# A GNN and FFN kernel: gather ring of 32 tiles, one landing semaphore per block, one ring of one-hots, one PSUM area for the three row parts

## The reference, cut to what matters

```python
x = x + gnn(layernorm(x), src, dst, ...)          # three of these layers, relu between them:
    agg  = segment_sum(h[src], dst, N)            # 200000 gathered rows a layer
    mean = agg / max(deg, 1)
    h    = h @ W_self + mean @ W_neigh + b
x = x + ffn(layernorm(x))                         # gelu(x @ w1 + b1) @ w2 + b2, times a routing
                                                  # weight, for the nodes with the largest weights
```

## Time and profile before

| what | us |
|---|---|
| median of the three runs | 6444.89 |
| the profiled execution, from its first to its last instruction (its span) | 7838.5 |
| POOL busy, of it the gathers | 4678.4, 4576.5 |
| PE busy (matmuls), weight loads | 4641.2, 2616.3 |
| DVE busy | 2368.1 |
| ACT busy | 896.4 |

### The profile page before, as it was taken

The page is one execution under the profiler, slowest core; times in us unless marked ns, Lnnn a source line. Parts: engine busy times, 40 slices in busy tenths (PEclk is TensorE's granted clock), DMA queues, the critical chain, the costliest instruction groups (busy, mean ns, idle before and its releaser), DMA issues.

```text
span 7838.5 us, 97787 instructions
## 1 busy us (share of the span) xinstructions
PE 4641.2 (59%) x19986; PEld 2616.3 (33%) x20208; DVE 2368.1 (30%) x5119; ACT 896.4 (11%) x2129; POOL 4678.4 (60%) x4762
## 2 busy tenths in 40 slices
PE   0445556666777544555555666544556667777884
PEld 0112223333444212222222223212334445555663
DVE  7111222233333211122233333211222233344446
ACT  3000000011111000000000000000111122223331
POOL 5666666666666566666666666666655555555551
PEclk9666677777888766667777777666767788888997
DMA  5444444444454444444445544444444444444444
GB/s 197 136 135 133 134 132 137 132 139 139 140 142 140 129 138 133 140 135 138 138 137 144 143 139 142 134 136 132 131 121 117 115 118 121 119 123 121 126 125 160
DMA packets 460486, 1056.21 MB, mean 135 GB/s; under 512 B 128083, under 2 KB 234279, under 8 KB 460455
## 3 DMA queue, kind: packets, MB, share of 16 engines
q0 software_dynamic: 301056, 925.15, 42.2%
q10 hardware_dynamic: 82364, 97.08, 3.5%
q1 hardware_dynamic: 77035, 33.62, 1.6%
HBM read 971.47 MB, written 84.02 MB: 135 GB/s over the span
## 4 chain that ended last, share of the span: by engine, by line
issue 38%; PE 32%; POOL 10%; another core or an unknown queue 8%; DVE 5%; DMA 2%; DVEq 2%; ACT 1%; SPq 1%; ACTq 0%; POOLq 0%
PE agg L613 12%; POOL gath L504 9%; PE agg_lo L614 6%; PE hid L657 5%; PE y L667 4%; DMA gath<-table,idx_ring 2%; PE hid L553 1%; PE y L553 1%; DVE resid L750 1%; PE hid L578 1%; DVEq L859 1%; DVE onehot L855 1%; DVEq L855 1%; PE agg_lo L603 0%
## 5 line engine op out<-in xcount | busy, mean ns | idle before, releaser
L504 POOL DMA_INDIRECT gath<-table,idx_ring x4704 | 4576.5, 973 | 2923.2 <-issue 1362.3
L613 PE MATMUL agg<-gath,onehot 128*128 x5778 | 2633.4, 478 | 2256.1 <-issue 1759.7
L855 DVE TENSOR_TENSOR onehot<-window_ids,dst_f 128x512 f32 x1464 | 1016.1, 694 | 3949.7 <-PE agg_lo L614 1434.4
L614 PE MATMUL agg_lo<-gath,onehot 128*128 x5856 | 1935.1, 330 | 380.5 <-issue 336.1
L613 PEld LDWEIGHTS agg<-gath,onehot 128*128 x5856 | 662.6, 113 | 3493.9 <-issue 3204.3
L614 PEld LDWEIGHTS agg_lo<-gath,onehot 128*128 x5856 | 660.1, 113 | 760.6 <-issue 576.0
L657 PE MATMUL hid<-featT,w_gnn 128*128 128x128 f32 x3136 | 485.4, 306 | 278.9 <-issue 277.4
L657 PEld LDWEIGHTS hid<-featT,w_gnn 128*128 128x128 f32 x3136 | 449.3, 218 | 311.9 <-issue 306.4
L667 PE MATMUL y<-w_sb,hidT 128*128 128x256 f32 x1568 | 392.5, 408 | 13.9 <-issue 10.9
L667 PEld LDWEIGHTS y<-w_sb,hidT 128*128 128x128 f32 x1568 | 317.1, 208 | 64.0 <-issue 15.1
L1103 ACT ACTIVATE featT<-tp 128x256 f32<-128x256 f32 x196 | 74.2, 379 | 2201.3 <-remote 1540.7
(11 more groups left out here) (129 smaller groups left out, 2462.0 us busy)
## 6 DMA issues: line engine op xcount, KB each, us to landing
gath<-table,idx_ring POOLq DMA_INDIRECT x4704
table<-split ACTq DMA_DIRECT2D x194, 192.0 KB
table<-gath ACTq DMA_DIRECT2D x24, 768.0 KB, 3.6
xb<-x ACTq DMA_DIRECT2D x97, 128.0 KB
yw_dram<-yw ACTq DMA_DIRECT2D x97, 128.0 KB
resid<-x SPq DMA_DIRECT2D x24, 512.0 KB, 7.3
gath<-yw_dram SPq DMA_DIRECT2D x12, 512.0 KB, 7.7
out<-gath ACTq DMA_DIRECT2D x12, 512.0 KB, 9.1
```

Of the source, the lines that this page charges most:

```text
L504: g.indirect_dma_start(gath[:, j, 0:PARTS * D], None, table[layer][:, :], bass.IndirectOffsetOnAxis(ap=idx_ring[:, h, j:j + 1], axis=0)).t ...
L613: mm(hi_mid, oh, tile_rows[:, :, 0:2 * D], start=False, **flags)
L614: last = mm(agg_lo[p][:, 0:lo_cols], oh, tile_rows[:, :, 2 * D:2 * D + lo_cols], start=False, **flags)
L855: v.tensor_tensor(onehot[p][:, bass.ds(slot, GROUP), :], window_ids[p][:].unsqueeze(1).to_broadcast([P, GROUP, P]), dst_f[:, bass.ds(tiles ...
```

## The change

- The ring of gathered rows has 32 slots (8 blocks). `idx_ring` keeps two halves of 16 tiles. `slots_free` starts at 8.
- The four gathers of a block raise one common semaphore, and SP makes one wait a block in place of four.
- The one-hots lie in one ring of 8 places, given out by pair (`(b + n) % 8`) in place of by block and parity. DVE's wait on `slots_free` is for one count more (`b + 2`).
- Each tile has three matmuls of 256 columns (the last 257 in layer 0), all into one PSUM area, in place of one of 512 and one of 256. One matmul with zeros opens the area, in place of two.
- `mean_done` and `aggregate_done` have one operation on the sum in place of three.
- To find room: `w_gnn2` lies in `hidT[0]` and is loaded by ACT after layer 0, ahead of `w1`; PE waits for it ahead of layer 1 (`w2g_loaded`). The 12 `fin` buffers all lie in `gath`; `part`, `trial`, `gains`, `sel` and `flags` lie in other buffers. `dst_f` has 1568 columns in place of 2052, and the last chunk's copy is shorter.

```diff
-RING = 16
+RING = 32
...
-    TURN_TILES = 2 * RING
+    TURN_TILES = RING
+    HALF_TILES = TURN_TILES // 2
+    HALF_BLOCKS = HALF_TILES // GROUP
...
-        onehot = [sb(f"onehot{p}", [P, RING, P], BF16) for p in range(2)]
+        onehot = sb("onehot", [P, RING, P], BF16)
...
+        w_gnn2 = hidT[0][:].rearrange("p k n -> p (k n)").rearrange("p (k n) -> p k n", k=KD)
...
-        agg = [psum(f"agg{p}", [P, 2, D]) for p in range(2)]
-        agg_lo = [psum(f"agg_lo{p}", [P, 512]) for p in range(2)]
+        agg = [psum(f"agg{p}", [P, 512]) for p in range(2)]
...
-                        for j in range(RING):
-                            sp.wait_ge(landed[j], it * 32 + 16 * (2 * layer * TURNS_PER_LAYER + h + 1))
-                            if j % GROUP == GROUP - 1:
-                                sp.sem_inc(rows_ready, 1)
+                        for q in range(h * HALF_BLOCKS, (h + 1) * HALF_BLOCKS):
+                            sp.wait_ge(landed[q], it * (16 * GROUP) + 16 * GROUP * (layer * TURNS_PER_LAYER + 1))
+                            sp.sem_inc(rows_ready, 1)
...
-                mm(hi_mid, zeros[:, 0:P], zeros[:, 0:2 * D], start=True, **free)
-                mm(agg_lo[p][:, 0:lo_cols], zeros[:, 0:P], zeros[:, 0:lo_cols], start=True, **free)
+                mm(agg[p][:, 0:lo_cols], zeros[:], ones_bf[:, 0:lo_cols], start=True, **free)
...
                     base = pe.snap((b % RING_BLOCKS) * GROUP)
+                    pair = pe.snap(((b + n) % RING_BLOCKS) * GROUP)
...
-                        oh = onehot[p][:, bass.ds(base, GROUP), :][:, j:j + 1, :]
+                        oh = onehot[:, bass.ds(pair, GROUP), :][:, j:j + 1, :]
...
-                        mm(hi_mid, oh, tile_rows[:, :, 0:2 * D], start=False, **flags)
-                        last = mm(agg_lo[p][:, 0:lo_cols], oh, tile_rows[:, :, 2 * D:2 * D + lo_cols],
-                                  start=False, **flags)
+                        for t in range(PARTS):
+                            cols = lo_cols if t == PARTS - 1 else D
+                            last = mm(agg[p][:, 0:cols], oh, tile_rows[:, :, t * D:t * D + cols], start=False,
+                                      **(flags if t == PARTS - 1 else free))
...
+            pe.wait_ge(w2g_loaded, 32)
...
-                    dve.wait_ge(slots_free, b + (layer * PADDED_BLOCKS + 1))
+                    dve.wait_ge(slots_free, b + (layer * PADDED_BLOCKS + 2))
...
-                for sums, added in ((agg_lo[p][0:r, 0:D], lo_added), (agg[p][0:r, 1, :], mid_added)):
-                    v.scalar_tensor_tensor(out=total, in0=sums, scalar=inv, in1=total, op0=ALU.mult,
-                                           op1=ALU.add).then_inc(added, 1)
-                    dve.wait_ge(added, n + (layer * NT + 1))
...
+            act.wait_ge(hT_ready, NT)
+            for h, w in enumerate((w_neigh[2], w_self[2])):
+                act.dma_start(w_gnn2[:, :, h * D:(h + 1) * D],
+                              w.rearrange("(k p) n -> p k n", p=P)).then_inc(w2g_loaded, 16)
             act.dma_start(w1_sb, w1.rearrange("(k p) n -> p k n", p=P)).then_inc(w1_loaded, 16)
```

More of the change, by code:

```diff
@@ L113, in gnn_ffn_program @@
         ident = sb("ident", [P, P])
[L114 to L115 removed]
+        zeros = sb("zeros", [P, P], BF16)
+        ones = sb("ones", [P, P + 2])
+        ones_bf = ones[:].bitcast(BF16)
         xb = [sb(f"xb{p}", [P, D]) for p in range(2)]
@@ L686, in total @@
                 pe.wait_ge(part_ready, i + 1)
-                mm(totals_ps, ones[:], part[:], start=True, stop=True).then_inc(total_ready, 1)
+                mm(totals_ps, ones[:, 0:P], part, start=True, stop=True).then_inc(total_ready, 1)
             last = NT - 1
@@ L851, in block_onehots @@
                 def block_onehots(b):
-                    slot, tiles = dve.snap((b % RING_BLOCKS) * GROUP), dve.snap(b * GROUP)
-                    dve.wait_ge(slots_free, b + (layer * PADDED_BLOCKS + 1))
-                    v.tensor_tensor(onehot[p][:, bass.ds(slot, GROUP), :],
+                    pair, tiles = dve.snap(((b + n) % RING_BLOCKS) * GROUP), nc.s_assert_within(
+                        dve.snap(b * GROUP), 0, (BLOCKS - 1) * GROUP,
+                        skip_runtime_bounds_check_because="blocks are counted from the sorted edges, below BLOCKS")
+                    dve.wait_ge(slots_free, b + (layer * PADDED_BLOCKS + 2))
+                    v.tensor_tensor(onehot[:, bass.ds(pair, GROUP), :],
                                     window_ids[p][:].unsqueeze(1).to_broadcast([P, GROUP, P]),
@@ L995, in _ @@
             link(v.memset(wanted, float(SELECTED)))
-            link(v.memset(part[:], 0.0))
+            link(v.memset(part, 0.0))
             totals = [0]
```

94 lines of the change are left out of this document (41 added, 53 removed).

## The result

The changed kernel takes **6554.94 us** in the median (6544.45 to 6560.63, 4 runs), the kernel before beside it 6445.62: ratio 1.0165, 95% interval 1.0153 to 1.0177. It is slower by 109 us. The forecast said 6400, with a range to 6540; the side that it gave 0.33 came, and further out than its 6529. So each ratio here is taken inside one job, and I compare traces of the pace of 6445 us alone, unless I say so. For that the kernel before was profiled once more (e0, 6435.4 us).

What follows compares the result with a forecast made beforehand. The prediction took POOL's gathers to bound the kernel (4704 at 1.25 us, 5880 us), with PE the bound late in layer 2. Sum: 6444.9 - 72 (ring) + 32 (third matmul) - 5 (DVE) = 6400 us; range 6280 to 6540.

Steps and rivals of the forecast that it cites:

- the 219.5 us over the gathers' floor: Run time beyond gathers and ends: 43.6 us layer changes, 40 DVE beside gathers, some 136 POOL's waits on PE.
- waits by bursts: POOL waiting while PE does 7 to 12 us of FFN work at once: 72 us of the 136.
- The ring of 32: Seven free blocks in place of three cover PE's FFN bursts: -72 us, bounds 0 and -136.
- The third matmul: Extra PE issue in late layer 2, up to 0.52 us a pair, taken at half, 0.25: +32 us.
- The 86 us for layer 2: Third matmul's cost at the full 0.52 us a pair, with PE the bound from window 35.
- the 8 us for layer 0: At the full price, layer 0's late windows would become PE-bound too, costing some 8 us.
- My test: Distance between two pairs' first weight loads late in layer 2: up to 2.2 us for the forecast, 2.5 for The slower rival.
- The gathers' pace: POOL's gathers keep 946 ns and 1.25 us each; the last doubt was that gathers running further ahead get slower.
- The DVE's two operations fewer: Two 484 ns operations less in each of 294 windows: -5 us, bounds 0 and -40.
- Landing semaphores and moved weights: SP's one wait a block and ACT's loads before layer 1, with 4.7 us of cover: 0.
- The slower rival: PE's issue becomes the bound in layer 2's `aggregate`: +94 us, -10 for bursts, 6529 us; chance 0.33.
- The profiled execution of 7838 us: Its 1613 us of POOL waiting, from PE standstills, was taken as mostly absent from the runs.

Runs made afterwards that it cites:

- e1: The changed kernel with the sums of before: two matmuls a tile (512 and 256 columns) in two PSUM areas, ring of 32 kept; 6457.85 us.
- e2: The kernel before, ring of 16, with only the sums changed: three matmuls of 256 columns in one PSUM area; 6536.43 us.
- e6: The changed kernel, with DVE's one-hots of a block held until POOL has begun the block before; 6474.92 us.
- e4: e1 with DVE's one-hots of a block held until POOL has begun the block before; 6399.46 us, ratio 0.9922 to 0.9955.
- e8: e2 without its third matmul: low part of the sums left out, two matmuls of 256 columns a tile; 6444.15 us.
- e12: The changed kernel with the window's ids, one input of the one-hot operation, moved from SBUF to PSUM; 8149.21 us, kernel before 7820.99 in that job.
- e15: e1 with each two-input one-hot operation replaced by four of one tensor and a scalar a partition; 6342.21 us, ratio 0.9829 to 0.9856.
- e11: e4 with DVE held one block longer, until POOL begins that very block; 6420.52 us, ratio 0.9950 to 0.9977.
- e9: The kernel before, ring of 16, with only e4's wait added; 6452.15 us, ratio 0.9999 to 1.0017.

## Why the prediction was wrong, step by step

**The failed step is the split of the 219.5 us over the gathers' floor.** It read: "a part of that is DVE beside it, and I put 40 us down to it", and from what was left, "The other 136 - 64 = 72 us are waits by bursts". e0 shows the split: lengthening of gathers is 4568.7 - 4704 * 0.946 = 119 us, of which 105 lie in gathers that begin under a one-hot, and POOL's waits beyond gaps and changes of layer are about 40 us, none of them in layers 0 and 1. So there were no 72 us of bursts to be won, and the DVE's share was nearly three times what I wrote down. The row for it stood there: the mean of 973 ns, which the prediction worked out, against the median of 946. 27 ns times 4704 is 127 us; I had the number and took 40 of it with no row for the 40. A remainder was called a wait.

That step alone doesn't make the miss. The forecast's terms add up to -45 us, the spans to +123. Of the 168 between them 61 are the ring's (-72 against -11), 49 the third matmul's (+32 against +81), 53 the gathers' pace (0 against +53) and 5 the DVE's.

**The ring of 32**, -72 expected: e1 shows waits 33 us less and 22 us more behind the last gather, since PE ends when it ends and POOL is only further ahead of it. That is 11 us, by this split; in e1's time it was more than taken back by gathers 31 us longer.

**The third matmul**, +32 at half its price: the full price a pair was right. I gave 0.52 us a pair as the upper end; in late layer 2 a pair takes 2.10 us in the changed kernel and 1.58 in e1, in the mean of 136 pairs each. "I take half, since half the pairs have the issue ahead of them" failed: about three in ten are the first of a window, and these too grew by 0.47 us in the mean, the later ones by 0.62. The 86 us for layer 2 came as 69 (e2), 75 (e6 against e4) and 81 (e1); the 8 us for layer 0 did not come, POOL waits no longer there. That the times agree so well with my 94 (+92 in e2, +97 against e1) is in part luck, since 22 to 30 us of them are longer gathers, which I had at nothing. My test named 2.2 us between pairs for the forecast and 2.5 for the rival; 2.31 to 2.34 lies between. Windows over 13.5 us were to refute me: 13.8 came.

**The gathers' pace**, held at 1.25 us: the last doubt I listed, gathers slower than that, was the right one, but for another reason. They are not slower by running further ahead; more of them begin under a one-hot (450 with 0.2 us or more left in e1 and 492 in the changed kernel, 411 in e0). Which part of the change moves the one-hots is not settled: e1, e2 and e8 each have 30 us of it, with different edits, and only the changed kernel has 53.

**The DVE's two operations fewer**, -5: nothing seen, and no run has them alone. e8 has them gone and is at the old time. **Landing semaphores and moved weights**, 0: right as far as seen, the changes of layer are 1 us shorter together, and at the first one PE still waits longest for SP's rows, the answer to the earlier trace rows:

```profile
2237.81 0.39 PE L597 MATMUL agg<-ones,zeros 128*128 128x256 bf16 x1 [6.73 <-DMA hidT<-w_self]
2245.25 1.03 PE L610 MATMUL agg<-gath,onehot 128*128 x4 [7.04 <-SPq L412]
```

The cover was there, though PE does wait for the moved weights first.

**The slower rival**, 6529: right in place and in the price of a pair, short by the gathers. With the parts as measured its sum is 6445 + 69 to 81 for the third matmul - 11 for the ring + 53 for the gathers = 6556 to 6568.

**The profiled execution of 7838 us**: that most of its waiting is not in the runs was right. "A thing of the profiled execution" was wrong: e12's job had it in timed runs. PE again stands with nothing that the profile shows ahead of it, as in e12:

```profile
6510.41 1.92 PE L610 MATMUL agg<-gath,onehot 128*128 x12 [0.71 <-issue]
6514.09 0.27 PE L610 MATMUL agg<-gath,onehot 128*128 x1 [1.76 <-issue]
```

## What to carry to other kernels

Before a remainder of the time is called a wait, take the mean of the bounding instruction from its median: mean less median, times the count, was 119 us here, three times the waits, and e15 won 102 us by it. Where POOL issues indirect gathers, let no DVE operation beside them read two tensors from SBUF: a scalar for one of them, or an operand in PSUM, took 95 to 106 us off the gathers of 4704. And where PE's issue is behind its array, as here with slots addressed by a register, PE pays for each load and matmul by count: don't split a matmul to save on something beside it unless the window's PE time has room for it.

## What the runs showed that I had not expected

- A gather that starts under a one-hot with two inputs from SBUF ends 818 ns behind it, within 2 to 3 ns, in five kernels. A one-hot that begins from 0.04 us ahead of the gather on costs it nothing; close around the start the one-hot is held instead, by up to 0.08 us.
- A matmul of 2 columns costs PE's issue as much as one of 256: 2.27 us a pair in both, 6553 and 6536 us in all.
- One wait more, on another engine's progress, can win 0.6% (e4) by setting only when an operation starts. It is fragile: a block later it won 0.4% (e11), with a ring of 16 nothing (e9).
- The same program has two paces, 6445 and 7720 to 7840 us, by the job. The order of versions isn't the same in both: e15's edit wins 1.6% at the one, and costs 1.5% with the ring of 16 at the other. What makes the second pace wasn't tried; on record its jobs ran on chips 2 and 0, the others on chips 5, 13 and 1, so job and chip can't be told apart.
